# Attention keys in three fp32r passes with their jobs in another order, and GpSimd's diagonals between two chunks of rows

## The reference

```python
# first cross attention; query = layernorm(x), key = value = ctx
q = query @ wq + bq;  k = key @ wk + bk;  v = value @ wv + bv     # 16 heads of 8
att = softmax(einsum('bhqd,bhkd->bhqk', q, k) / SCALE)
out = einsum('bhqk,bhkd->bhqd', att, v) @ wo + bo
...
# second cross attention; 16 heads of 64; keys and values from [layernorm(ctx) * w + b, latn]
weight = softmax(einsum('bhld,bhnd->bhln', q * scale, k * scale))
out = einsum('bhln,bhnd->bhld', weight, v) @ Wo
```

## Time and profile before

| | |
|---|---|
| median of 3 runs | 1756.41 us (1752.18 to 1757.27) |
| profiled execution | 1755.67 us |
| its span, first to last instruction | 1753.7 us |
| PE, DVE, ACT, POOL busy | 91%, 72%, 54%, 34% of the span |
| mean granted TensorE clock | 0.963 of full speed |
| idle time in the first attention that ends with DVE's low keys, ahead of the key product on PE | 10.1 us |
| idle time that ends with POOL's diagonal, ahead of the normalising product on PE | 13.1 us |

### The profile page before, as it was taken

One profiled execution on the slowest core, in us unless ns is written; L12 is line 12 of the kernel. 1 busy time (PEld: TensorE's weight loads), 2 busy tenths in 40 slices (PEclk: granted clock), 3 DMA queues, 4 the chain that ended last, 5 costly groups with the idle time before them and its releaser, 6 DMA issues. The chain is left out here.

```text
span 1753.7 us, 34517 instructions
## 1 busy us (share of the span) xinstructions
PE 1594.2 (91%) x13452; PEld 1399.0 (80%) x13452; DVE 1264.4 (72%) x2838; ACT 955.0 (54%) x1788; POOL 603.8 (34%) x855
## 2 busy tenths in 40 slices
PE   6999999999997899379999999999999999999964
PEld 4766766767666788269999999999999999999843
DVE  7677767676673777367777777787777877777587
ACT  3565655655653344146556566666665566656442
POOL 2001000110101222154665455744666455743110
PEclk8999999999998999679999999999999999999986
DMA  6534545435320011211010000001010010000000
GB/s 161 144 98 93 136 123 116 95 98 128 76 58 1 1 73 73 94 51 31 20 32 19 26 32 20 32 13 32 20 32 31 14 32 20 32 1 1 1 3 9
DMA packets 32689, 90.90 MB, mean 52 GB/s; under 512 B 8552, under 2 KB 17424, under 8 KB 32528
## 3 DMA queue, kind: packets, MB, share of 16 engines
q1 hardware_dynamic: 32528, 88.71, 19.1%
HBM read 40.43 MB, written 8.91 MB: 28 GB/s over the span
## 5 line engine op out<-in xcount | busy, mean ns | idle before, releaser
L389 DVE TENSOR_TENSOR c_p_lo<-c_turn_ps,c_p_hi 128x512 fp32r<-128x512 f32 x384 | 264.3, 688 | 170.3 <-ACT c_p_hi L338 167.2
L338 ACT ACTIVATE c_p_hi<-c_turn_ps 128x512 fp32r<-128x512 f32 x384 | 228.4, 595 | 233.7 <-PE c_turn_ps L246 232.5
L1027 DVE TENSOR_REDUCE a_chunk_max<-a_side_ps 128x1 f32<-128x512 f32 (+1 forms) x416 | 260.8, 665 | 96.0 <-PE a_side_ps L778 95.7
L356 ACT ACTIVATE c_prob<-c_score_ps,c_neg_max 128x836 f32<-128x836 f32 (+1 forms) x256 | 245.3, 958 | 41.3 <-DVE c_neg_max L427 39.5
L2353 PE MATMUL c_pv_ps<-c_p_hi,c_v_lo 128*128 128x256 f32 (+1 forms) x896 | 261.1, 291 | 0.0
L380 DVE TENSOR_REDUCE c_chunk_max<-c_score_ps 128x1 f32<-128x836 f32 (+2 forms) x384 | 257.1, 721 | 4.7 <-PE c_score_ps L276 4.7
L246 PE MATMUL c_turn_ps<-consts,c_prob 128*128 128x128 f32 (+1 forms) x1792 | 246.9, 275 | 11.5 <-DVE c_p_lo L389 11.3
L2354 PE MATMUL c_pv_ps<-c_p_hi,c_v_hi 128*128 128x256 f32 (+1 forms) x896 | 250.3, 279 | 0.0
L2355 PE MATMUL c_pv_ps<-c_p_lo,c_v_hi 128*128 128x256 f32 (+1 forms) x896 | 250.1, 279 | 0.0
L938 ACT ACTIVATE a_prob<-a_st_ps 128x1024 f32<-128x1024 f32 (+1 forms) x224 | 214.1, 959 | 53.5 <-PE a_st_ps L762 52.8
L246 PEld LDWEIGHTS c_turn_ps<-consts,c_prob 128*128 128x128 f32 (+1 forms) x1792 | 206.3, 140 | 33.4 <-DVE c_p_lo L389 18.7
(11 more groups left out here) (337 smaller groups left out, 2804.7 us busy)
## 6 DMA issues: line engine op xcount, KB each, us to landing
a_stack<-a_k_hi SPq DMA_DIRECT2D x128, 200.1 KB, 4.2
a_stack<-a_k_lo SPq DMA_DIRECT2D x64, 200.1 KB, 4.2
a_ctx<-in_ctx_dram SPq DMA_DIRECT2D x16, 768.0 KB
c_ctx<-in_ctx_dram SPq DMA_DIRECT2D x16, 768.0 KB
absorbed_queries<-b_q_out SPq DMA_DIRECT2D x16, 512.0 KB, 3.3
c_q_raw<-absorbed_queries SPq DMA_DIRECT2D x16, 512.0 KB, 3.3
w<-in_L_ffn_w_dram SPq DMA_DIRECT2D x2, 512.0 KB
fold_raw<-in_L_xattn_Wkv_dram SPq DMA_DIRECT2D x2, 512.0 KB
```

Of the source, the lines that this page charges most:

```text
L338: last = nc.scalar.activation(p_hi[u][:, 4 * c:4 * c + 4, P * j:P * j + P], turn_ps[c % 2][:].rearrange("p (t q) -> p t q", t=4), ACT.Copy)
L356: nc.scalar.activation(prob[s % 2][:, probs_of[c]], score_ps[:, cols], ACT.Exp, bias=neg_max[:, s % 2:s % 2 + 1], accum_out=sums[:, (s // ...
L389: last = nc.vector.tensor_tensor(p_lo[u][part], turn_ps[c % 2][:].rearrange("p (t q) -> p t q", t=4), p_hi[u][part].bitcast(F32), ALU.subt ...
L1027: nc.vector.reduce_max(out, rows, AX_X).then_inc(side_taken, 1)
```

## The change

In the first attention a table gives the scratch jobs another order: values and turned context alternate in the even octet, and the keys stand in steps 1, 3, 5 and 6 of the odd one with q in step 2. The key product of the three full chunks is made of three fp32r products, high by high, high by low and low by high part of wk and of the turned context. GpSimd makes these parts: wk's once, the context's chunk by chunk as it is turned. The fourth chunk stays in plain fp32. In the second attention `normed_rows` is cut in two functions: GpSimd centres all rows and finishes chunks 0 and 1 before the diagonal, chunks 2 and 3 behind it. Buffers of layer 0 are placed at the other side of the memory, and three buffers of later parts are allocated after the first attention.

```diff
@@ -461,25 +461,26 @@
 STEPS = (TILES_A + 1) // 2
 UNITS = 3 * QUAD + 1
 HALF_DMAS = 6
+SPLIT_CHUNKS = 3
 ONES_AT = 96
 STACK_ROWS = ONES_AT + QUAD
 V_COLS = 17
 
 
+JOB_ORDER = (("v", 0), ("v", 1), ("ctx_t", 0), ("v", 2), ("ctx_t", 1), ("v", 3), ("ctx_t", 2),
+             ("ctx_t", 3), ("k", 0), ("q", 0), ("k", 1), None, ("k", 2), ("k", 3))
+
+
 def job_at(n, s):
 
 
-    b = n // 2
-    if n % 2 == 0:
-        what, c, b = ("v", s, b + 1) if s < CHUNKS else ("ctx_t", s - CHUNKS, b + 2)
-    elif s == 0:
-        what, c, b = "ctx_t", 3, b + 2
-    elif s <= CHUNKS:
-        what, c, b = "k", s - 1, b + 2
-    elif s == CHUNKS + 1 and b < CHUNKS:
-        what, c, b = "q", b, 0
-    else:
+    job = JOB_ORDER[STEPS * (n % 2) + s]
+    if job is None:
         return None
+    what, c = job
+    if what == "q":
+        return ("q", n // 2, 0) if n // 2 < CHUNKS else None
+    b = n // 2 + (1 if what == "v" else 2)
     return (what, c, b) if b < BATCH else None
 
 
@@ the buffers @@
+        ctx_hi, ctx_lo = (sb(n, [P, SPLIT_CHUNKS * BANK], F32R) for n in ("ctx_hi", "ctx_lo"))
+        wk_hi, wk_lo = sb("wk_hi", [P, D], F32R), sb("wk_lo", [P, D], F32R)
@@ -723,6 +727,15 @@
                 nc.gpsimd.tensor_tensor(g.act_t[:, u, :, b * SEQ:b * SEQ + SEQ], raw[n % 2][:].rearrange("p (i q) -> p i q", i=2),
                                         rden[n % 2][:].rearrange("p (i q) -> p i q", i=2), ALU.mult).then_inc(heads_done, 1)
 
+            def split_context(c, b):
+                cols = quad_chunk(c, CTX)
+                pool.wait_ge(job_taken, number["ctx_t", c, b] + 1)
+                if b > 2:
+                    pool.wait_ge(job_ready, number["k", c, b - 1] + 1)
+                nc.gpsimd.tensor_copy(ctx_hi[:, cols], ctx_t[:, cols]).then_inc(ctx_high, 1)
+                pool.wait_ge(ctx_high, SPLIT_CHUNKS * (b - 2) + c + 1)
+                nc.gpsimd.tensor_tensor(ctx_lo[:, cols], ctx_t[:, cols], ctx_hi[:, cols].bitcast(F32), ALU.subtract).then_inc(ctx_split, 1)
+
             nc.gpsimd.memset(half[:], -0.5).then_inc(zeroed, 1)
             nc.gpsimd.memset(bv_rows[:], 0.0).then_inc(zeroed, 1)
             nc.gpsimd.memset(wo_rows[:], 0.0).then_inc(zeroed, 1)
@@ -738,7 +751,14 @@
                 block_diagonal(n)
             nc.gpsimd.memset(stack[ONES_AT:STACK_ROWS, 1].bitcast(F32), 1.0).then_inc(ones_set, 1)
             pool.wait_ge(ones_set, 2)
+            pool.wait_ge(k_loaded, 32)
+            nc.gpsimd.tensor_copy(wk_hi[:], wk[:]).then_inc(wk_high, 1)
+            pool.wait_ge(wk_high, 1)
+            nc.gpsimd.tensor_tensor(wk_lo[:], wk[:], wk_hi[:].bitcast(F32), ALU.subtract).then_inc(wk_split, 1)
             for n in range(OCTETS):
+                if n % 2 == 0 and n // 2 + 2 < BATCH:
+                    for c in range(SPLIT_CHUNKS):
+                        split_context(c, n // 2 + 2)
                 if n + 4 == LATE_AT:
                     pool.wait_ge(q_split, 2 * GROUPS)
                 if n + 4 < OCTETS:
@@ -828,8 +848,15 @@
                     for i, (rows, _) in enumerate(tiles[4 * c:4 * c + 4]):
                         last = nc.tensor.transpose(scratch[:, P * i:P * i + rows], ctx_in[0:rows, 4 * c + i, :], g.consts[0:rows, C_IDENT:C_IDENT + rows])
                 elif what == "k":
-                    c = job[1]
-                    last = nc.tensor.matmul(scratch[:, 0:widths[c]], wk[:], ctx_t[:, quad_chunk(c, CTX)], start=True, stop=True)
+                    c, b = job[1:]
+                    cols = quad_chunk(c, CTX)
+                    if c < SPLIT_CHUNKS:
+                        pe.wait_ge(wk_split, 1)
+                        pe.wait_ge(ctx_split, SPLIT_CHUNKS * (b - 2) + c + 1)
+                        for i, (weights, keys) in enumerate(((wk_hi, ctx_hi), (wk_hi, ctx_lo), (wk_lo, ctx_hi))):
+                            last = nc.tensor.matmul(scratch[:, 0:widths[c]], weights[:], keys[:, cols], start=(i == 0), stop=(i == 2))
+                    else:
+                        last = nc.tensor.matmul(scratch[:, 0:widths[c]], wk[:], ctx_t[:, cols], start=True, stop=True)
                 elif what == "q":
                     last = nc.tensor.matmul(scratch[0:ONES_AT], wq3[:, job[1]].rearrange("p i r -> p (i r)"), xn_t[:, BANK:2 * BANK], start=True, stop=True)
                 else:
@@ -2255,14 +2282,17 @@
             pool.wait_ge(t.rstd_done, b + 1)
             nc.gpsimd.tensor_tensor(t.shift[:], t.shift[:], t.rstd[:], ALU.mult).then_inc(t.shift_done, 1)
 
-        def normed_rows(eng, ops, b, m, first, waits):
+        def centred_rows(eng, ops, b, waits):
 
             wait_apart(eng, t.shift_done, b + 1, waits)
             for i in range(FULL + 1):
                 rows = lay.tiles[i][0]
                 ops.tensor_scalar(t.ctx[0:rows, i, :], t.ctx[0:rows, i, :], t.rstd[0:rows, i:i + 1], t.shift[0:rows, i:i + 1],
                                   ALU.mult, ALU.add).then_inc(t.centred, 1)
-            for c in range(CHUNKS):
+
+        def weighted_rows(eng, ops, b, chunks):
+
+            for c in chunks:
                 n = 4 if c < 3 else 1
                 rows, tiles = (P if c < 3 else TAIL), slice(4 * c, 4 * c + n)
                 eng.wait_ge(t.centred, (FULL + 1) * b + 4 * c + n)
@@ -2306,9 +2336,11 @@
                 pool.wait_ge(lay.own.scores_ready, (b - 1) * PAIRS * CHUNKS)
             split_queries(pool, b, (m + 1) % 2)
             factors(pool, b)
-            normed_rows(pool, nc.gpsimd, b, (m + 1) % 2, first, t.pool_waits)
+            centred_rows(pool, nc.gpsimd, b, t.pool_waits)
+            weighted_rows(pool, nc.gpsimd, b, range(2))
 
         def pool_split(pool, k, kind, m):
+            weighted_rows(pool, nc.gpsimd, 2 * k + m + 1, range(2, CHUNKS))
             split_rows(pool, nc.gpsimd, 2 * k + m + 1, (m + 1) % 2, kind == "first" and m == 0, t.pool_waits)
 
         lay.pool_start, lay.pool_prepare, lay.pool_split = pool_start, pool_prepare, pool_split
...
@@ -2539,18 +2572,18 @@
         g = Named()
         g.x_tok = sb("x_tok", [P, TOK_TILES, D])
         g.consts = sb("consts", [P, C_END])
-        g.lat_rows = sb("lat_rows", [SEQ, BATCH, D])
-        g.wvo = sb("wvo", [P, HEADS, D])
-        g.rest_1 = rest_1_buffers(sb)
         with ExitStack() as layer_0:
             def sb_0(name, shape):
-                return layer_0.enter_context(nc.sbuf_tensor(name, shape, F32))
+                return layer_0.enter_context(nc.sbuf_tensor(name, shape, F32, side="right"))
 
             g.act_t = sb_0("act_t", [P, QUADS, 2, TOKENS])
             g.wo_half = sb_0("wo_half", [P, QUADS, 2, D])
             g.rest_0 = rest_0_buffers(sb_0)
             g.fold_raw = sb_0("fold_raw", [P, 4 * PAIRS, P])
             cross_attention_0(nc, g, dram)
+            g.lat_rows = sb("lat_rows", [SEQ, BATCH, D])
+            g.wvo = sb("wvo", [P, HEADS, D])
+            g.rest_1 = rest_1_buffers(sb)
             g.qk = sb_0("qk", [P, HEADS, D])
             rest_of_layer_0(nc, g, dram)
         cross_attention_1(nc, g, dram)
```

More of the change, by code:

```diff
@@ L589, in cross_attention_0 @@
         first_values, first_taken = sem("first_values"), sem("first_taken")
+        wk_high, wk_split, ctx_high, ctx_split = (sem(n) for n in ("wk_high", "wk_split", "ctx_high", "ctx_split"))
         ctx.enter_context(nc.allow_non_contiguous_dma(reason="vectors: one element per partition"))
@@ L2443, in dve_start @@
             dve.wait_ge(t.loaded, 32)
-            normed_rows(dve, nc.vector, 0, 0, True, t.waits)
+            centred_rows(dve, nc.vector, 0, t.waits)
+            weighted_rows(dve, nc.vector, 0, range(CHUNKS))
             for c in range(CHUNKS):
```

## The result

The change takes the kernel from a median of 1756.44 us to **1725.74 us** (four runs, 1724.65 to 1726.07), a ratio of 0.9829 with a 95% interval of 0.9814 to 0.9845. That is 30.7 us less; the forecast was 1717, 39.1 us less. The time lies in the range, with 8.7 us missing from the gain. The profiled execution took 1726.07 us, its span 1724.1 us, against 1753.7 before.

The account below looks back on a forecast made before the run. Both attentions were taken as bound by TensorE and what it waits for. Second attention 14.5 plus first attention 28.1 minus stack 3.5 made 39.1 us less than the 1756.41 us median: 1717 us, range 1704 to 1735.

Parts of the forecast that it names:

- Second attention, 14.5 us: Slot 5 of odd batches: TensorE's wait for GpSimd's diagonal goes, 8 x 1.81 = 14.5 us less.
- rival (c): Second attention gives nothing, as chunk 2's transposition or the late load takes the wait's place: 1731 us; chance 0.05.
- The key product, 0.07 us a job: First attention: three fp32r products take 0.70 us for the fp32 job's 0.77; all 42 jobs would save 3 us.
- Odd octets, 14.19 us: First attention: the new job order brings an odd octet from 16.31 to 14.19 us, or 15.1 with q.
- Even octets, 15.25 us: First attention: an even octet waits 0.3 us for the last maxima, loses a 0.4 us wait: 15.25 for 15.38.
- The stack, 3.5 us: First attention: six transfers after the last low keys land with little room; 0.25 us a pair charged, 3.5 us.
- The wait of 0.2 us in each pair: Sign expected: a wait of 0.2 us or so for the stack at step 4's side product in an even octet.
- its sign of being wrong: First attention: the side product waiting for the stack by over 1 us would show the prediction wrong.
- Rival (a): The stack becomes the bound, its sixth transfer issued 1.3 us later: 14 x 1.3 = 18 us, 1735 us; chance 0.15.
- GpSimd at no cost: First attention: three casts and three subtractions a pair, at most 7.7 us on GpSimd, busy 3.0 of 31.7 us.
- Rival (d): GpSimd's splits block VectorE in the first attention: slower, 1825 us at full price; chance 0.03.
- Rival (b): First attention: VectorE holds TensorE nowhere any more, 0.95 us a pair, 13 us less, 1704 us; chance 0.12.

Follow-up runs that it names:

- passes_only: The changed kernel with the three fp32r key passes but the scratch jobs in the order of before; 1733.57 us.
- even_old: The changed kernel with the even octet's jobs in their old places (values in steps 0 to 3, context 0 to 2 in steps 4 to 6); 1727.56 us.
- both_again: Repeat of both_moved, the same kernel, run beside the change itself; 1718.98 us against 1727.27 us.
- both_moved: The changed kernel with the odd octet's keys sooner and, in the even octet, the narrow value job in step 4 and context 1 in step 5; 1719.36 us.

## Why the forecast came out as it did

- **Second attention, 14.5 us:** right. 1.9 us a slot for 1.81 in the odd batches, 15.1 in all; nothing took the wait's place, so rival (c) is refuted.
- **The key product, 0.07 us a job:** mechanism right, size off: 0.16 (both by the rows and by passes_only), 42 x 0.16 = 7 us for 3. Inside the octet 0.70 was right for the three products; what was missed is that the scores behind three short passes take 0.48 us instead of 0.56. The Trainium skill (FP8 and Floating Point Precision, "TensorE Precision Notes") has true FP32 as four passes; the estimate from it, with 0.23 us a pass, was a saving of 0.22 a job. The measured 0.16 lies between that and my 0.07, nearer to the skill's.
- **Odd octets, 14.19 us:** 14.36. The waits of steps 2, 4 and 5 came where they were followed. Step 5 was mis-sized by 0.18: from the second side product to the key job it takes 0.34 us where I gave 0.23, and the wait ends 0.07 later. With q the octet is 15.3 for 15.1.
- **Even octets, 15.25 us: this is the step that failed.** It said that the even octet "waits 0.3 us for the last maxima and loses a wait of 0.4". The first came (0.17 us in step 0). The wait was not lost: the side products of step 6 still take 1.02 us for 0.55. even_old shows the old order's steps intact, and with the new order step 6 waits 0.23 us more. I had followed DVE through the odd octet step by step and settled the even one in a sentence. Against the forecast that is 0.56 x 14 = 7.8 us, most of what is missing; the odd octets make up 2.5 more and the stack 0.7, and the second attention gives 0.6 back. That makes 10.4 us; between the spans 9.5 are missing, and between the medians 8.7.
- **The stack, 3.5 us:** 4.2 us in sum, but not as 0.25 us in each pair. It is nothing in ten octets and 1 us in four, and the cause (the instruction packets) was in none of my cases. That the sum came near 3.5 is luck, since it has another cause than the one forecast. The room that I counted as 0.1 us was really 0.5, which kept it small. The wait of 0.2 us in each pair, a sign that the prediction named, did not come; its sign of being wrong, a wait of over 1 us, was just met in octet 24 (1.04). Rival (a), which had later issues in every pair, did not come.
- **GpSimd at no cost:** right; a cast takes 0.61 us and a subtraction 1.28, 5.7 us a pair of the 7.7 allowed, and twice as much costs under 1 us. Rival (d) is refuted with it. Rival (b) is refuted by the 0.2 us waits in steps 2, 4 and 5 that are still there.

**The spread of the timed runs** is 7 to 8.5 us for the versions with the keys sooner, 1.4 and 3.8 for the change, up to 6.4 for the kernel before. It goes with the granted clock of the whole run: both_again has 1714.74 us at 0.968 and 1723.24 at 0.959, both_moved 1715.74 at 0.964 and 1723.90 at 0.958. Their two traces, of one and the same kernel, show where. Octets 2 to 29 take 419.2 us in both; from the last octet's first score product to the first one of the second attention it is 223.8 us in both_moved and 231.9 in both_again. Below is the stretch from 512 to 760 us (PE busy, clock, DMA share, GB/s), first of both_moved, then of both_again:

```profile
512.00:760.00 248.00, 186.74 (x1354) 0.88 0.14 52
```

```profile
512.00:760.00 248.00, 187.50 (x1306) 0.84 0.15 52
```

The change puts no work into that stretch (227.8 us before, 227.5 after), so the 30.7 us stand; but it can move a single run by 8 us, more than most of the differences between the experiments. Hence the octets are the better measure here. Why the clock falls more often there in one run than in the next stays open.

## What to carry to other kernels

When an order of jobs is changed, follow the slower engine through every step of the whole period; the half that seems untouched lost 6 us here. A transfer that is due with half a microsecond of room is late when another packet falls into its last part. Moving its source sooner gives it room, and moving the keys and one narrow job (a table of 14 entries) was worth 8.3 us more. But part of that came by the packets' new places: ask of an absent wait whether the room covered a late landing, as in octet 26 of the kernel before, or whether there was none. The wait that struck a few octets out of many equal ones had its cause outside the loop's own work. And where one stage of a long kernel wanders with the clock, compare the stage that was changed, not the whole time.

## What the hardware showed that was not expected

- Packets of a kind that the profile calls instruction come while the program runs: 107 of 16384 bytes on q8, in the first attention one per about 255 of TensorE's instructions. The four that made the change's stack late took 0.88 to 0.96 us each, others up to 1.6. When one starts 6.3 to 6.7 us behind the last low keys, late in the last of a batch's six transfers, the landing comes 9.2 to 9.65 us behind these keys in all 29 cases, and in three of 11 cases with a packet at 7.4 to 7.5; all other landings come at 8.0 to 8.7, mostly 8.0 to 8.1. The kernel before had that once (9.31 us, ahead of octet 26), hidden since its side product stands at 11.85.
- 128 instructions more at the head of TensorE's program move these collisions to other iterations. For one kernel their places come again (4, 14, 22 and 24 in both traces of the change); from kernel to kernel none to four of 14 batches are hit.
- Three fp32r products of 512 columns in a row take 0.69 us, and the short scores behind them start closer (0.48 us for four, 250.18 to 250.66) than behind a job of turned context (0.56, 283.99 to 284.55 in the earlier trace rows). With one fp32 product in their place, job and scores together take 1.33 us for 1.17.
- One kernel's stretch between the attentions took 223.8 us at a mean granted clock of 0.89 and 231.9 at 0.85 in two executions.
